# Transposed one-hots six groups ahead, sums added two groups behind, keys in blocks of two groups

## The reference

```
xn = layernorm(x)
h  = xn @ W, 4 heads of 64;  a_src, a_dst = h . att_src, h . att_dst        (per node and head)
logit(e) = leaky_relu(a_src[src] + a_dst[dst], 0.2)
out[n] = sum over edges into n of exp(logit - shift[n]) * h[src]  /  the sum of the exps
x = x + relu(out + bias) + linear_attention(xn)
x = x + mixture of 8 experts (2 per node, gelu, 256 -> 1024 -> 256) of layernorm(x)
```

## The kernel before

| Engine | Step n |
|---|---|
| ScalarE | off n+4; exponentials n+2 (wait for logits n+2); relu n+4 (waits until spread n+2 is done) |
| TensorE | spread n+3 and its extra work (waits for relu n+3); sum n (waits for weighing n and add n-4) |
| VectorE | weighing n; logits n+2, first part (waits for spread and gather n+2); one-hot n+5; extra work; second part; add n-1 (waits for sum n-1); third part; node work |

## Time and profile before

### The profile page before, as it was taken

The page is one execution under the profiler, slowest core; times in us unless marked ns, Lnnn a source line. Parts: engine busy times, 40 slices in busy tenths (PEclk is TensorE's granted clock), DMA queues, the critical chain, the costliest instruction groups (busy, mean ns, idle before and its releaser), DMA issues. The chain is left out here.

```text
span 1184.8 us, 18797 instructions
## 1 busy us (share of the span) xinstructions
PE 963.2 (81%) x5226; PEld 829.5 (70%) x5227; DVE 493.3 (42%) x1357; ACT 400.5 (34%) x1107; POOL 558.0 (47%) x574
## 2 busy tenths in 40 slices
PE   6917778788879788676677675599999999999995
PEld 5807556566657567565565563599899999999995
DVE  5607645557536556555546566711111111111110
ACT  4504322223323322432433332433333333333331
POOL 2270566666666666666666620423333333333332
PEclk8967787777786778777777687799999999999998
DMA  6331333434444434434443423956655656566561
GB/s 194 105 106 56 107 109 108 126 108 126 123 129 122 123 107 138 128 108 131 116 133 107 131 65 123 325 162 182 176 179 176 177 174 181 177 177 178 176 177 20
DMA packets 73069, 164.84 MB, mean 139 GB/s; under 512 B 11152, under 2 KB 40485, under 8 KB 72883
## 3 DMA queue, kind: packets, MB, share of 16 engines
q0 software_dynamic: 30336, 69.57, 23.7%
q1 hardware_dynamic: 42115, 94.07, 23.3%
q10 hardware_dynamic: 560, 0.52, 0.1%
HBM read 147.00 MB, written 17.12 MB: 139 GB/s over the span
## 5 line engine op out<-in xcount | busy, mean ns | idle before, releaser
L561 POOL DMA_INDIRECT gathered<-h_table,src_row x416 | 399.1, 959 | 246.9 <-issue 116.7
L881 PE MATMUL bank<-gathered,one_hot 128*128 128x260 f32 x832 | 280.1, 492 | 13.4 <-issue 8.2
L824 PEld LDWEIGHTS bank<-adc,w_sb 128*128 128x128 f32 x832 | 135.7, 240 | 154.0 <-issue 147.8
L881 PEld LDWEIGHTS bank<-gathered,one_hot 128*128 128x128 f32 x832 | 195.7, 247 | 63.9 <-issue 29.0
L824 PE MATMUL bank<-adc,w_sb 128*128 x832 | 132.5, 287 | 123.8 <-ACT w_sb L658 105.3
L1669 ACT ACTIVATE hiddenT<-bank,b_slot 128x128 f32<-128x128 f32 x432 | 123.5, 369 | 252.6 <-PE bank L1704 252.6
L1704 PEld LDWEIGHTS bank<-xgT,acc 128*128 128x128 f32 x1728 | 203.6, 194 | 2.7
L1647 POOL DMA_INDIRECT out<-y,add_index x54 | 86.0, 1593 | 253.0 <-DVE y L1759 125.2
L1704 PE MATMUL bank<-xgT,acc 128*128 128x128 f32 x1728 | 203.8, 277 | 0.0
L1722 PE MATMUL bank<-w_sb,hiddenT 128*128 x864 | 197.0, 381 | 0.0
L1722 PEld LDWEIGHTS bank<-w_sb,hiddenT 128*128 128x128 f32 x864 | 159.9, 190 | 22.1 <-issue 1.6
(11 more groups left out here) (238 smaller groups left out, 693.5 us busy)
## 6 DMA issues: line engine op xcount, KB each, us to landing
acc<-in_L_ffn_W SPq DMA_DIRECT2D x54, 1024.0 KB, 6.5
w_sb<-key_table SPq DMA_DIRECT2D x26, 512.0 KB
w_sb<-in_L_ffn_W SPq DMA_DIRECT2D x8, 1024.0 KB, 11.9
gathered<-h_table,src_row POOLq DMA_INDIRECT x416
h_table<-acc SPq DMA_DIRECT2D x25, 130.0 KB, 2.0
out<-w_sb SPq DMA_DIRECT2D x5, 512.0 KB
xn_table<-w_sb SPq DMA_DIRECT2D x5, 512.0 KB
xs<-in_x SPq DMA_DIRECT2D x3, 640.0 KB, 10.7
```

The lines of the kernel that those rows point to most:

```text
L561: pool.indirect_dma_start(gathered[:, r, j, :], None, h_table, bass.IndirectOffsetOnAxis(ap=src_row[:, t:t + 1], axis=0)).then_inc(gather_ ...
L824: mm = pe.matmul(ad_bank[r % ADS][:, j * 2 * HEADS:(j + 1) * 2 * HEADS], one_hotT[:, r % 2, j, :], flat(adc[:, bass.ds(k, 1), :]), start=T ...
L881: mm = pe.matmul(sum_bank[r % SUMS][:, 0:ROW], one_hot[:, r, j, :], gathered[:, r, j, :], start=(j == 0), stop=(j == G - 1))
```

## The change

The transposed one-hots get four buffers (HOTS) for two, and ScalarE makes them six groups ahead (FAR_ON) for four, six of them ahead of step 0. VectorE adds sum n-2 in step n, not sum n-1. Key blocks hold two groups (256 KB) for four; the extra space of the one-hots is what the keys give up. The node work's waits and the places of SyncE's stores are shifted to fit.

```diff
--- before.py
+++ after.py
@@ -41,7 +41,9 @@
 NB = NT
 HALF = P // 2
 KEYS = 2
-KBLK = 4
+KBLK = 2
+HOTS = 4
+FAR_ON = 6
 AHEAD = KEYS * KBLK
 G = 4
 RING = 8
@@ -203,13 +205,13 @@
             z = sb(scope, "z", [P, 2, G, HEADS])
 
             late = flat(w2_sb[:, (NX - 2) * KF:NX * KF, :])
-            one_hotT = late[:, 0:2 * G * P].rearrange("p (a j c) -> p a j c", a=2, j=G)
-            key_offs = late[:, 2 * G * P:3 * G * P]
-            key_part = late[:, 3 * G * P:3 * G * P + AHEAD * G * P // 2]
+            one_hotT = late[:, 0:HOTS * G * P].rearrange("p (a j c) -> p a j c", a=HOTS, j=G)
+            key_offs = late[:, HOTS * G * P:(HOTS + 1) * G * P]
+            key_part = late[:, (HOTS + 1) * G * P:(HOTS + 1) * G * P + AHEAD * G * P // 2]
             keys = key_part.bitcast(I16).rearrange("p (a g e) -> p a g e", a=KEYS, g=KBLK)
             past_rows = key_part[0:EQ, 0:G * P].bitcast(I32)
             key_rows = key_part[0:EQ, G * P:G * P + G * P // 2].bitcast(I16)
-            held = late[:, 3 * G * P + AHEAD * G * P // 2:]
+            held = late[:, (HOTS + 1) * G * P + AHEAD * G * P // 2:]
             w_q = held[:, 0:KD * HID].rearrange("p (k n) -> p k n", k=KD)
             w_o = held[:, KD * HID:KD * HID + D]
 
@@ -483,9 +485,9 @@
                         sp.sem_inc(waited, 1)
                         for q in range(NGRP // KBLK):
                             for k in range(INSIDE):
-                                if q == ready_of(k, 11) // KBLK + 1:
+                                if q == ready_of(k, 13) // KBLK + 1:
                                     keep_x(c, k)
-                                if q == ready_of(k, 11) // KBLK + 2:
+                                if q == ready_of(k, 13) // KBLK + 3:
                                     keep_xn(c, k)
                             send_keys(c, q)
                         keep_xn(c, INSIDE - 1)
@@ -655,7 +657,7 @@
                     def hotT(n, r):
 
                         act.wait_ge(key_off, n + 1)
-                        act.activation(one_hotT[:, r % 2, :, :].rearrange("p a b -> p (a b)"), key_offs, ACT.Relu,
+                        act.activation(one_hotT[:, r % HOTS, :, :].rearrange("p a b -> p (a b)"), key_offs, ACT.Relu,
                                        bias=ones[:, 0:1], scale=-1.0).then_inc(hotT_ready, 1)
 
                     def deviation(c, k):
@@ -684,14 +686,14 @@
                         act.activation(gathered[:, r, :, D:ROW], z[:, r % 2, :, :], ACT.Exp).then_inc(exp_ready, 1)
 
                     def step(c, n, s, r, ahead):
-                        if ahead >= 4:
-                            off(c, n + 4, s + 4)
+                        if ahead >= FAR_ON:
+                            off(c, n + FAR_ON, s + FAR_ON)
                         if ahead >= 2:
                             exps(n + 2, s + 2, (r + 2) % RING)
-                        if ahead >= 4:
-
-                            act.wait_ge(ad_ready, n + 3)
-                            hotT(n + 4, r + 4)
+                        if ahead >= FAR_ON:
+
+                            act.wait_ge(ad_ready, n + FAR_ON - HOTS + 1)
+                            hotT(n + FAR_ON, r + FAR_ON)
                         for k in range(INSIDE):
                             if s == ready_of(k, 4):
                                 deviation(c, k)
@@ -700,10 +702,10 @@
                                     normalise_again(c, k, part)
 
                     with act.Fori(0, passes) as c:
-                        for r in range(4):
+                        for r in range(FAR_ON):
                             off(c, c * NGRP + r, r)
-                            if r >= 2:
-                                act.wait_ge(ad_ready, c * NGRP + r - 1)
+                            if r >= HOTS:
+                                act.wait_ge(ad_ready, c * NGRP + r - HOTS + 1)
                             hotT(c * NGRP + r, r)
                         exps(c * NGRP, 0, 0)
                         exps(c * NGRP + 1, 1, 1)
@@ -821,7 +823,7 @@
                         k = pe.snap(win_reg, min_val=0, max_val=NW - 1)
                         pe.wait_ge(hotT_ready, n + 1 + AHEAD)
                         for j in range(G):
-                            mm = pe.matmul(ad_bank[r % ADS][:, j * 2 * HEADS:(j + 1) * 2 * HEADS], one_hotT[:, r % 2, j, :],
+                            mm = pe.matmul(ad_bank[r % ADS][:, j * 2 * HEADS:(j + 1) * 2 * HEADS], one_hotT[:, r % HOTS, j, :],
                                            flat(adc[:, bass.ds(k, 1), :]), start=True, stop=True)
                         return mm
 
@@ -1171,7 +1173,7 @@
                         low, high = PIECES[k]
                         b = min(k, INSIDE) if k < len(PIECES) - 1 else len(BATCHES) - 1
                         at = low - BATCHES[b][0]
-                        last = c * NGRP + min(ready_of(k, 0), NGRP - 1)
+                        last = c * NGRP + min(ready_of(k, -1), NGRP - 1)
                         dve.wait_ge(added, last * 2 + 4)
                         dve.reciprocal(rden[:, low:high, :], acc[:, low:high, D:ROW]).then_inc(den_ready, 1)
                         stores = c * ((len(BATCHES) + 1 - b % 2) // 2) + b // 2
@@ -1225,10 +1227,11 @@
                     def last_steps(c, n, s, r):
 
                         weigh(n, r)
-                        add_sums(n - 1, s - 1, r - 1)
+                        add_sums(n - 2, s - 2, r - 2)
                         scale(c, INSIDE + 1)
                         weigh(n + 1, r + 1)
                         merge(c, INSIDE + 1)
+                        add_sums(n - 1, s - 1, r - 1)
                         logits(n + 2, r + 2, 0)
                         if s + 2 in GATES:
                             low, high = BATCHES[GATES[s + 2]]
@@ -1262,8 +1265,8 @@
                             add_bias(low, high, gates_at(r + 2)[:, 0:high - low, :])
                         if ahead >= 2:
                             logits(n + 2, (r + 2) % RING, 1)
-                        if s > 0:
-                            add_sums(n - 1, s - 1, (r - 1) % RING)
+                        if s > 1:
+                            add_sums(n - 2, s - 2, (r - 2) % RING)
                         if ahead >= 2:
                             logits(n + 2, (r + 2) % RING, 2)
                         node_work(c, s)
```

## The result

The kernel with the change takes 1186.56 us (median of 15 runs, 1181.59 to 1195.42), the kernel before in the same comparison 1195.8 us (1190.1 to 1203.04): a ratio of 0.9928, interval 0.9907 to 0.9948. That is 8.6 us faster by the ratio, where 52 were forecast. The profiled execution took 1185.52 us.

What follows compares the result with a forecast made beforehand. The prediction took the loop to be bound by waits, no engine full. Its terms, -48 - 6 + 0.9 + 0.9 = -52.2 us, took the profiled 1186.7 to 1134.5 us, given as 1144 us for the runs' median; range 1104 to 1193 us.

Steps and rivals of the forecast that it cites:

- late stretch: In the loop: TensorE's results come some 6 us after its rows end; VectorE and GpSimd are let go together.
- three chains: In the loop: late results, half clock, and the order of relu, spread, weighing and sum; the change attacks only the last.
- Part 1: Loop, one-hots six groups ahead: TensorE's 33 waits for relus (102.2 us) go, gaining 1.45 us each, -48 us.
- Part 2: Loop, sums added two groups behind: VectorE's idle before the adds mostly goes; ends 0 and 49 us, taken -6 us.
- Part 3: Key transfers of two groups: 52 instead of 26, landing in 3.2 us with about 3 us of cover, 0 us.
- Part 4: Start: two more abs and relu pairs before the first exponentials, +0.9 us; end: one more add before the last logits, +0.9.
- B: Late results own the loop: 1189 us, chance 0.22; sign: L1155's waits grow by what L1142's lose, groups still 5.9 us.
- A: GpSimd becomes the loop's bound, under 5.0 us a group; all 97.4 us of its waiting go: 1100 us, chance 0.14.
- C: Loop slower by TensorE's clock: half-clock share 70%, 1238 us, chance 0.11; sign: clock under 0.7 from 124 us to loop's end.
- D: Keys late in the loop: a landing of 8.4 us instead of 3.2 holds 50 blocks, 1244 us, chance 0.03.

Runs made afterwards that it cites:

- e12: The changed kernel as it is, on the quick chip (kernel before: 1050 to 1063 us): 1050.33 us, 0.9952 of the kernel before.
- e13: The changed kernel without its gathers of groups 8 to 103, on the slow chip: 957.53 us, 0.7998 of the kernel before.
- e17: The changed kernel, GpSimd waiting before every second group of gathers until the group before has landed, slow chip: 1180.5 us, 0.9923 of the kernel before.
- experiment 7: The kernel before with one-hots six ahead in four buffers and key blocks of two groups, sums still added one group behind, slow chip: 0.994.
- e3: The changed kernel with three extra matmuls (128x124) per group before TensorE's wait for the weighing, quick chip: 1051.02 us, 0.9945 of the kernel before.
- e16: The changed kernel with gathers of groups 8 to 103 moving 208 bytes a row instead of 1040, slow chip: 1191.48 us, 0.9932 of the kernel before.
- e15: The changed kernel with at most six groups of gathers in flight in place of eight, slow chip: 1184.62 us, 0.9883 of the kernel before.

## Why the prediction was wrong

The loop, from first weighing to last add, and what stands around it, in us (spans of the profiled executions):

```
                       first weighing   loop     behind   span
before, slow              118.37        602.6    463.9   1184.8
after, slow               120.03        600.5    463.3   1183.8
after, quick (e12)         84.64        499.6    463.6   1047.8
one ring, slow (e13)      122.09        371.8    463.7    957.6
pauses, slow (e17)         96.20        619.5    461.1   1176.7
```

**Reading the profile.** That the loop is one of waits, with no full engine, was right, and the late stretch was seen and named. What I made of it was wrong: three chains that "share the time", of which the change attacks the last. On this chip they are mostly one chain. The late results decide, and the waits for relus and sums lay largely inside the time that they were late. The trace of before shows it: in 18 of the 33 waits for a relu, with 89 of the 102.2 us, a stand of VectorE or GpSimd for TensorE's results ends within the wait.

**Part 1 (-48 us): the step that failed.** The mechanism came as described: no wait for L660 is left, and the sum's wait is put down to the weighing. The price was wrong. I took 33 waits times a gain of 1.45 us as if each moved the end of the loop. Part 1 alone gave 0.994 (0.9911 to 0.9968), some 7 us in place of 48, and the time it took away came back as TensorE's later wait for the weighing (65.4 us, experiment 7), and VectorE's for the logits (130.6 after 97.3 us). A place where a result is awaited is no cost of its own when the release doesn't depend on how early the waiter comes.

**Part 2 (-6 us).** Alone it gave 0.9897 (0.9866 to 0.9928), some 12 us: about twice the forecast, and as much as the whole change within the noise. VectorE's idle before the adds went as said (134.0 to 21.5), and as said the next wait is L1157. The two parts don't add up, so by these medians they remove in part the same time. Of the two ends, 0 and 49 us, the lower one was near.

**Part 3 (0).** Right: 52 transfers, and all that an abs (L655) ever waits for one is 0.2 us, although the landing had 3.5 us in the trace of e3 (256 KB) where I took 3.2.

**Part 4 (+0.9, +0.9).** From the first gather to the first weighing 68.5 us in place of 67.0: +1.5. From the landing of the last gather to the last add 21.5 in place of 23.2: no loss at the end.

**Rivals.** B came true, and it has its sign: L1157's waits grew by 106.9 while L1144's lost 112.5, with 5.9 us a group. I had given it 0.22 against 0.50, on the ground that 102 us of TensorE's idle were outside the late stretches. The trace of before refutes that ground for 89 of them (above), and part 1 alone, which takes all 102 away and gains 7, shows what it was worth. A holds on the quick chip: 5.0 us a group, GpSimd without a break, and neither the change (0.9952) nor a higher clock (e3) does more there. GpSimd's waits for sums, forecast to fall from 97 to some 45 us, stayed (93.5 us without the one before group 8). C did not come: the clock from 124 to 696 us is 0.75 after 0.76. D did not either.

**The cause underneath.** On the slow chip TensorE's results come late, and its matmuls slower, while GpSimd issues gathers without a pause (from about the eighth in the filling, at 60 us). In the loop those that are waited for are there some 2.5 us after GpSimd stopped; in the filling some come earlier, in the midst of the gathers. Without the later gathers the late stretches go (e13), with pauses they go (e17), with fewer bytes or buffers they stay (e16, e15). The period is then GpSimd's, 12 x 1.25 = 15.0 us and 2.8 of pause for three groups, 5.9 each, and none of the three reorderings of the other engines' work (part 1, part 2, both) changed the whole by more than some 12 us. Pauses of my own cost the same time over. Nor is it the loading of instructions from memory that ends the stand in the filling: between 60 and 97.5 us of the first result's trace no queue but the gathers' moves data, and TensorE goes on at 96.35. The 9 us that the change does give are not explained by this period; which step gives them stays open, as does why one chip does this and the other doesn't, and by what path GpSimd reaches TensorE. The Trainium skill (SBUF — State Buffer, "SBUF: two separate sides") says that TensorE never waits on anyone for its port. That GpSimd's issuing delays TensorE's results is shown by e13 and e17; whether a port has to do with it no run here shows, so the measurement neither bears out that sentence nor refutes it.

## What to carry to other kernels

Before pricing a wait, ask whether its end depends on when the waiter comes: if two engines are let go within a microsecond of each other (0.8 us here), long after the rows of the engine they wait for have ended, look for what a third engine stopped doing just before, and price the change by that engine's rhythm. Test parts singly, as their waits may be one and the same time. And look at the start of a kernel for the plain form of what is tangled in its loop: 32 gathers beside a run of matmuls showed here what 104 groups hid.

## What the runs showed that I had not expected

The same kernel takes 1055 us on one chip and 1190 on another, and all of the 136 us between the traces of the changed kernel stand where GpSimd issues gathers in long runs: 35.4 between the first gather (51.5 us in both) and the loop, 100.9 in the loop, and 0.3 us of difference in the 463 us behind it, though GpSimd issues 108 indirect transfers there too. In the filling the slow chip's results of TensorE are up to 34 us late, and a few of its matmuls come 0.7 us apart and more, where they come every 0.12 us before. The granted clock is 0.51 there (the first result, 65 to 90 us), and 0.86 on the quick chip in the same stretch. The lower mean clock of the slow chip (0.84 against 0.89) goes with the gathers too: without them both loops have 0.96 (124 to 430 us).
